# Epsilon of four norms as a third triple in VectorE's aggregate, the last norm's factor and shift side by side, and a new order of work

## The reference

```
h = patches(16x16) @ W.T + b; class token in front; + positions    # 32 x 37 tokens x 256 ("tok")
h = h + gated_scan(norm(norm0(h)))       # two norms in a row, gate = sigmoid, h_t = (1-z) h_{t-1} + z c_t, + its own input
h = h + ffn(norm1(h))                    # ternary W_fc (256->1024), exact gelu, norm with weights, ternary W_proj
h = h + attention(norm2(h))              # rope on q and k, causal softmax over 37 tokens, output product
h = h + quantised_linear(norm3(h))       # x / scale, round, clip to +-127, ternary weights, + bias
norm(x) = (x - mean) / sqrt(var + 1e-5)  # over the 256 features of a token
```

## Time and profile before

| | |
|---|---|
| median of 3 runs | 163.69 us (163.63 to 164.32) |
| profiled execution | 163.71 us, span of its instructions 161.9 us |
| TensorE busy | 148.2 us (91%) |
| VectorE | 136.1 us (84%) |
| GpSimd | 120.3 us (74%) |
| ScalarE | 109.0 us (67%) |
| mean granted clock of TensorE | 0.974 |
| chain that ended last | TensorE 70%, GpSimd 13%, VectorE 6%, waiting to issue 6% |

### The profile page before, as it was taken

The page is one execution under the profiler, slowest core; times in us unless marked ns, Lnnn a source line. Parts: engine busy times, 40 slices in busy tenths (PEclk is TensorE's granted clock), DMA queues, the critical chain, the costliest instruction groups (busy, mean ns, idle before and its releaser), DMA issues.

```text
span 161.9 us, 3532 instructions
## 1 busy us (share of the span) xinstructions
PE 148.2 (91%) x1043; PEld 129.5 (80%) x1043; DVE 136.1 (84%) x396; ACT 109.0 (67%) x264; POOL 120.3 (74%) x214
## 2 busy tenths in 40 slices
PE   7979999999998999999999999999999999697541
PEld 7969999788997887879888989988998798574220
DVE  0767679999999999999979799888988896896871
ACT  3765359736448899999998958498827637276330
POOL 1068978968927466878889988869899888988830
PEclk9999999999999999999999999999999999999955
DMA  5999992000030000000000000000000000001323
GB/s 171 340 392 392 379 417 109 4 0 2 0 130 4 2 0 2 0 4 0 0 4 2 0 4 0 2 0 0 4 0 0 0 6 2 2 10 46 87 81 81
DMA packets 6026, 10.84 MB, mean 67 GB/s; under 512 B 1841, under 2 KB 3448, under 8 KB 5752
## 3 DMA queue, kind: packets, MB, share of 16 engines
q1 hardware_dynamic: 6008, 10.62, 18.7%
HBM read 9.40 MB, written 1.21 MB: 66 GB/s over the span
## 4 chain that ended last, share of the span: by engine, by line
PE 70%; POOL 13%; DVE 6%; issue 6%; ACT 2%; DVEq 0%; ACTq 0%; POOLq 0%
PE bank L428 37%; PE bank L508 5%; PE bank L575 5%; PE bank L509 4%; PE bank L510 4%; PE bank L517 3%; POOL small L1186 3%; PE bank L435 3%; POOL qk L1251 2%; POOL small L1181 2%; POOL residual L1282 2%; POOL small L1191 2%; PE bank L549 1%; PE bank L629 1%; DVE residual L1160 1%
## 5 line engine op out<-in xcount | busy, mean ns | idle before, releaser
L1186 POOL TENSOR_TENSOR small<-small,powers 111x1 f32<-111x1 f32 (+3 forms) x55 | 33.3, 606 | 3.7
L1181 POOL TENSOR_SCALAR small<-small 111x1 f32<-111x1 f32 (+1 forms) x55 | 24.2, 441 | 15.0 <-DVE small L892 11.3
L428 PE MATMUL bank<-pj,gt_hi 128*111 128x256 f32 (+1 forms) x88 | 22.3, 293 | 0.0
L428 PE MATMUL bank<-pj,gt_lo 128*111 128x256 f32 (+1 forms) x88 | 21.3, 281 | 0.0
L1202 POOL TENSOR_TENSOR x_lo<-x_raw,x_hi 128x666 fp32r<-128x666 f32 (+1 forms) x9 | 12.8, 1434 | 10.8 <-ACT x_hi L721 10.8
L508 PE MATMUL bank<-wt_hi,x_hi 128*111 128x256 f32 (+1 forms) x66 | 19.4, 294 | 1.4 <-DVE h L998 1.1
L510 PE MATMUL bank<-wt_hi,x_lo 128*111 128x256 f32 (+1 forms) x66 | 18.6, 282 | 0.0
L509 PE MATMUL bank<-wt_lo,x_hi 128*111 128x256 f32 (+1 forms) x66 | 18.6, 282 | 0.0
L428 PE MATMUL bank<-fc,n1t_hi 128*111 128x512 f16 (+1 forms) x44 | 16.7, 380 | 0.0
L428 PE MATMUL bank<-fc,n1t_lo 128*111 128x512 f16 (+1 forms) x44 | 16.6, 378 | 0.0
L428 PEld LDWEIGHTS bank<-pj,gt_hi 128*111 128x111 f32 (+1 forms) x88 | 15.1, 171 | 0.3 <-DVE residual L1088 0.2
(11 more groups left out here) (139 smaller groups left out, 478.9 us busy)
## 6 DMA issues: line engine op xcount, KB each, us to landing
x_raw<-x_in SPq DMA_DIRECT2D x10, 333.0 KB, 6.4
w_fc<-w_fc_in SPq DMA_DIRECT2D x1, 1024.0 KB, 10.2
w_pj<-w_pj_in SPq DMA_DIRECT2D x1, 1024.0 KB, 12.2
...
```

What stands on the lines that cost most here:

```text
L428: last = mm(out, a, b, start=(n == 0), stop=(n == len(pairs) - 1))
L1181: return nc.gpsimd.tensor_scalar(small[0:rows(i), i, out:out + 1], small[0:rows(i), i, value:value + 1], factor, add, ALU.mult, ALU.add)
L1186: return gt(small[0:rows(i), i, r:r + n], small[0:rows(i), i, ve:ve + n], powers[0:rows(i), 0:n], ALU.pow)
```

## The change

Four things:
1. The statistics get a standing third triple (norm 0 a fourth, too): count 0, mean 0 and count x variance of 256 eps. The aggregate over 9 (12) values then gives var + eps at once, and the 55 additions on GpSimd go. Norm 0 has two aggregates per tile instead of one: over three triples for the inner factor, over four for the outer. The factor (1 + eps)^-1/2 that is left over goes into gamma (w_gamma on VectorE, before ScalarE's and VectorE's w_gate). The standing triples are written by five memsets on GpSimd at the start.
2. In norm 3 the shift no longer waits for the factor: it is mean x power x (-1/scale), by a second column operand, issued right behind the factor.
3. ScalarE's n3 waits for both.
4. The lists of the four engines are written anew (shown are the head and the end of each).

```diff
 ORDER = {
     "tensor": """
-        warm:0 tok:0 w_pos:0 tok:1 tok:2 tok:3 w_gate:0 tok:4 t0:0 tok:5 t0:1 tok:6 t0:2 tok:7 w_fold:0 t0:3
...
-        attend:4 turn:6 value:5 qk:11 value:6 t3:1 attend:5 turn:7 attend:6 value:7 score:8 score:9 t3:2
-        attend:7 value:8 score:10 turn:8 t3:3 t3:4 out:0 attend:8 value:9 out:1 turn:9 t3:5 attend:9 t3:6
-        turn:10 value:10 out:2 attend:10 out:3 out:4 t3:7 out:5 out:6 out:7 t3:8 out:8 t3:9 out:9 t3:10 out:10""",
+        warm:0 w_pos:0 tok:0 tok:1 tok:2 tok:3 w_gate:0 tok:4 t0:0 tok:5 t0:1 tok:6 t0:2 tok:7 w_value_bias:0
+        t0:3 t0:4 w_ternary:0 w_fold:0 w_fold:1 t0:5 gate:0 gate:1 gate:2 tok:8 t0:6 t0:7 tok:9 tok:10 gate:3
...
+        qk:6 attend:0 score:3 qk:7 value:1 turn:1 proj:10 turn:2 t2:8 value:2 t2:9 attend:1 turn:3 attend:2
+        score:4 value:3 t2:10 score:5 attend:3 qk:8 qk:9 turn:4 value:4 score:6 qk:10 attend:4 score:7 qk:11
+        turn:5 value:5 t3:0 turn:6 value:6 attend:5 turn:7 value:7 attend:6 t3:1 value:8 score:8 score:9
+        attend:7 out:0 t3:2 turn:8 score:10 attend:8 turn:9 out:1 value:9 t3:3 t3:4 attend:9 turn:10 value:10
+        out:2 t3:5 out:3 attend:10 t3:6 out:4 t3:7 out:5 out:6 t3:8 out:7 out:8 t3:9 out:9 t3:10 out:10""",
     "scalar": """
-        split:0 w_tok:0 w_tok:1 split:1 split:2 split:3 split:4 w_gate:0 split:5 split:6 split:7 w_qk:0 split:8
...
-        value:4 turn:5 n3:2 score:7 t3:0 turn:6 n3:3 value:5 value:6 value:7 turn:7 n3:4 score:8 t3:1 n3:5 t3:2
-        value:8 t3:3 turn:8 n3:6 score:9 value:9 t3:4 turn:9 n3:7 score:10 turn:10 value:10 n3:8 n3:9 t3:5 t3:6
-        t3:7 t3:8 n3:10 t3:9 t3:10""",
+        split:0 w_tok:0 split:1 w_tok:1 split:2 split:3 split:4 split:5 split:6 w_gate:0 split:7 t0:0 w_qk:0
...
+        turn:4 score:6 score:7 turn:5 value:5 turn:6 value:6 turn:7 value:7 t3:0 n3:3 n3:4 value:8 t3:1 score:8
+        turn:8 n3:5 score:9 turn:9 n3:6 t3:2 value:9 score:10 t3:3 turn:10 t3:4 n3:7 t3:5 value:10 n3:8 t3:6
+        t3:7 n3:9 t3:8 n3:10 t3:9 t3:10""",
     "vector": """
-        w_ones:0 split:0 w_tok:0 w_tok:1 split:1 split:2 w_pos:0 h0:0 stats0:0 mean0:0 w_gate:0 w_small:0 h0:1
...
-        attend:3 sinv:5 clip:0 clip:1 score:7 stats3:3 sbias:6 round:0 round:1 mean3:3 rope:4 attend:4 sbias:7
-        stats3:4 mean3:4 clip:2 rope:5 sinv:6 sinv:7 attend:5 stats3:5 attend:6 mean3:5 stats3:6 clip:3 round:2
-        score:8 score:9 sbias:8 mean3:6 round:3 attend:7 clip:4 stats3:7 sinv:8 round:4 score:10 clip:5 mean3:7
-        sbias:9 sbias:10 out:0 clip:6 attend:8 stats3:8 round:5 round:6 mean3:8 out:1 sinv:9 attend:9 clip:7
-        sinv:10 stats3:9 mean3:9 clip:8 out:2 attend:10 round:7 stats3:10 out:3 mean3:10 out:4 out:5 round:8
-        out:6 out:7 clip:9 clip:10 round:9 round:10 out:8 out:9 out:10""",
+        w_ones:0 split:0 w_tok:0 w_tok:1 split:1 w_pos:0 split:2 h0:0 stats0:0 h0:1 w_small:0 mean0:0 stats0:1
+        h0:2 stats0:2 h0:3 mean0:1 w_gamma:0 n0:0 mean0:2 w_gate_bias:0 w_gate:0 n0:1 t0:0 h0:4 stats0:3 mean0:3
...
+        score:7 stats3:4 sbias:7 mean3:4 rope:5 clip:2 round:1 round:2 sinv:6 attend:5 stats3:5 sinv:7 mean3:5
+        attend:6 clip:3 clip:4 round:3 score:8 sbias:8 stats3:6 score:9 attend:7 sbias:9 mean3:6 sinv:8 stats3:7
+        out:0 round:4 clip:5 score:10 attend:8 sbias:10 mean3:7 out:1 clip:6 round:5 sinv:9 sinv:10 stats3:8
+        mean3:8 attend:9 stats3:9 out:2 clip:7 round:6 round:7 mean3:9 out:3 attend:10 out:4 clip:8 out:5
+        stats3:10 mean3:10 round:8 out:6 out:7 clip:9 clip:10 round:9 round:10 out:8 out:9 out:10""",
     "gpsimd": """
-        w_tok:0 split:3 split:4 h0:0 split:5 split:6 h0:1 split:7 h0:2 split:8 h0:3 h0:4 h0:5 split:9 split:10
...
-        attend:0 vbias:9 rope:3 biased:0 proj:10 attend:1 vbias:10 attend:2 attend:3 biased:1 rope:4 attend:4
-        biased:2 biased:3 rope:5 attend:5 attend:6 biased:4 attend:7 attend:8 biased:5 biased:6 attend:9
-        biased:7 biased:8 attend:10 biased:9 biased:10""",
+        w_tok:0 split:3 split:4 split:5 h0:0 split:6 h0:1 h0:2 split:7 split:8 h0:3 h0:4 h0:5 h0:6 h0:7 split:9
...
+        attend:0 square:10 rope:3 proj:10 biased:0 attend:1 attend:2 biased:1 attend:3 biased:2 rope:4 vbias:9
+        attend:4 rope:5 attend:5 biased:3 biased:4 attend:6 biased:5 attend:7 vbias:10 biased:6 attend:8
+        biased:7 attend:9 biased:8 attend:10 biased:9 biased:10""",
 }
...
+SQ_EPS = LN_EPS * LN_EPS / (1.0 + LN_EPS)
+GROUP, GROUPS = 3, 4
...
-    stats = m.own("stats", [4, 2, 8], F32)
+    stats = m.own("stats", [4, 2, GROUP * GROUPS], F32)
...
+                act.wait_ge(s["gamma_ready"], 1)
                 for k in range(KD):
-                    go(wg_hi[:, k, :], w_gate[:, k, :], ACT.Copy, scale=packed[:, GAMMA + k:GAMMA + k + 1])\
+                    go(wg_hi[:, k, :], w_gate[:, k, :], ACT.Copy, scale=derived[:, D_GAMMA + k:D_GAMMA + k + 1])\
...
                 act.wait_ge(s["nb3_ready"], i + 1)
+                act.wait_ge(s["rq_ready"], i + 1)
...
-                        dve.wait_ge(s[f"mv{norm}_ready"], i - 1)
+                        dve.wait_ge(s[f"mv{norm}_ready"], (i - 1) * (2 if norm == 0 else 1))
+                    if i == 0:
+                        dve.wait_ge(s["eps_groups_ready"], 5)
...
-                    nc.vector.bn_aggr(col(i, normed[norm][2], 2), stats[0:rows(i), norm, i % 2, 0:6])\
-                        .then_inc(s[f"mv{norm}_ready"], 1)
+                    groups = stats[0:rows(i), norm, i % 2, :]
+                    if norm == 0:
+                        nc.vector.bn_aggr(col(i, MV0_SQ, 2), groups[:, 0:3 * GROUP]).then_inc(s["mv0_ready"], 1)
+                        nc.vector.bn_aggr(col(i, MV0, 2), groups[:, 0:4 * GROUP]).then_inc(s["mv0_ready"], 1)
+                    else:
+                        nc.vector.bn_aggr(col(i, normed[norm][2], 2), groups[:, 0:3 * GROUP])\
+                            .then_inc(s[f"mv{norm}_ready"], 1)
...
+            def w_gamma(_i):
+                dve.wait_ge(s["dma_packed"], 16)
+                ts(derived[:, D_GAMMA:D_GAMMA + KD], packed[:, GAMMA:GAMMA + KD], (1.0 + LN_EPS) ** -0.5, None, ALU.mult)\
+                    .then_inc(s["gamma_ready"], 1)
...
+                dve.wait_ge(s["inv_scale_ready"], 1)
+                ts(derived[:, D_NEG_INV_SCALE:D_NEG_INV_SCALE + 1], derived[:, D_INV_SCALE:D_INV_SCALE + 1], -1.0, None,
+                   ALU.mult).then_inc(s["neg_inv_scale_ready"], 1)
...
-            def scaled(i, out, value, factor, add):
-                return nc.gpsimd.tensor_scalar(small[0:rows(i), i, out:out + 1], small[0:rows(i), i, value:value + 1],
-                                               factor, add, ALU.mult, ALU.add)
-
-            def power(i, ve, r, n=1):
-
-                return gt(small[0:rows(i), i, r:r + n], small[0:rows(i), i, ve:ve + n], powers[0:rows(i), 0:n],
+            def power(i, mv, r, n=1):
+
...
+                nc.gpsimd.memset(stats[:, :, :, 2 * GROUP:3 * GROUP - 1], 0.0).then_inc(s["eps_groups_ready"], 1)
+                nc.gpsimd.memset(stats[:, 0, :, 3 * GROUP:4 * GROUP - 1], 0.0).then_inc(s["eps_groups_ready"], 1)
+                for norm, group, added in ((0, 2, SQ_EPS), (0, 3, LN_EPS - SQ_EPS)):
+                    nc.gpsimd.memset(stats[:, norm, :, GROUP * group + 2:GROUP * group + 3], D * added)\
+                        .then_inc(s["eps_groups_ready"], 1)
+                nc.gpsimd.memset(stats[:, 1:4, :, 3 * GROUP - 1:3 * GROUP], D * LN_EPS)\
+                    .then_inc(s["eps_groups_ready"], 1)
...
-                pool.wait_ge(s["mv0_ready"], i + 1)
-                scaled(i, VE0, MV0 + 1, 1.0, LN_EPS).then_inc(s["ve0_ready"], 1)
-                scaled(i, VE0 + 1, MV0 + 1, 1.0 + LN_EPS, LN_EPS * LN_EPS).then_inc(s["ve0_ready"], 1)
-                pool.wait_ge(s["ve0_ready"], 2 * i + 2)
-                power(i, VE0, R0, 2).then_inc(s["r0_ready"], 1)
+                pool.wait_ge(s["mv0_ready"], 2 * i + 2)
+                power(i, MV0, R0, 2).then_inc(s["r0_ready"], 1)
 
             def h1_(i):
                 pool.wait_ge(s["mv1_ready"], i + 1)
-                scaled(i, VE1, MV1 + 1, 1.0, LN_EPS).then_inc(s["ve1_ready"], 1)
-                pool.wait_ge(s["ve1_ready"], i + 1)
-                power(i, VE1, R1).then_inc(s["r1_ready"], 1)
+                power(i, MV1, R1).then_inc(s["r1_ready"], 1)
                 pool.wait_ge(s["r1_ready"], i + 1)
                 shift(i, NB1, MV1, R1, "nb1_ready")
 
...
                 pool.wait_ge(s["mv3_ready"], i + 1)
-                scaled(i, VE3, MV3 + 1, 1.0, LN_EPS).then_inc(s["ve3_ready"], 1)
-                pool.wait_ge(s["ve3_ready"], i + 1)
-                power(i, VE3, R3).then_inc(s["r3_ready"], 1)
+                power(i, MV3, R3).then_inc(s["r3_ready"], 1)
                 if i == 0:
                     pool.wait_ge(s["inv_scale_ready"], 1)
 
                 pool.wait_ge(s["r3_ready"], i + 1)
                 gt(small[0:rows(i), i, RQ:RQ + 1], small[0:rows(i), i, R3:R3 + 1],
```

(8 more changed lines are left out.)

103 lines of the change are left out of this document (50 added, 53 removed).

## The result

In runs side by side the changed kernel took 171.02 us in the median (168.83 to 172.12, 4 runs), the kernel before 164.00 (163.63 to 164.37, 4 runs): a ratio of 1.0345, interval 1.0244 to 1.0446. The forecast was 162.2 us in a range up to 164.5. It was wrong in sign and by 8.8 us.

A forecast was written before the change was run, and what follows sets the result against it. TensorE's products bound 12 to 130 us, latencies, mainly GpSimd's, the 32 us tail. Ideal -2.35 + 0.2 = -2.15 us, low bound -0.2; -1.5 us taken from 163.71 gave 162.2 us, range 160.9 to 164.5.

The forecast's parts named there:

- "New: idle from 6.1 to 7.9", the head at +0.5 us: Head: TensorE waits for w_pos's operands until 7.9 us, so tok:1 starts at 11.3 against 10.79, +0.5 us.
- Rival (b): Head: TensorE's gap keeps its clock low, 1.7 to 3.3 us more, giving 164.7 us; chance 0.12.
- "ScalarE's w_gate behind w_gamma and two splits. Nothing.": Head: moving ScalarE's w_gate costs nothing, as gates need wg_hi over 10 us later; without that cover, 1.5 us.
- "Between 12 and 130 us I cost their going at nothing": Middle: removing GpSimd's epsilon additions gains nothing there, since TensorE's products hide them.
- "0.2 for the late aggregates": VectorE after 30 us: three tiles' extra norm 0 aggregates are charged 0.2 us, the rest hidden.
- The aggregates: VectorE, norm 0: 11 more aggregates cost 0.8 to 1.9 us in all, 0.07 each at least; longer reads nothing.
- Rival (d): VectorE: the third triple slows 44 aggregates by up to the 0.42 us bound, +3 us or more; chance 0.03.
- The negated factor and the memsets: VectorE's small negated factor goes with the aggregates' charge; five GpSimd memsets before 2 us cost nothing.
- The tail at -2.35, taken as -1.5: Tail: GpSimd's shift of attend:10 ends at 151.65 instead of 154.00, -2.35 us; -1.5 us taken overall.
- rival (a): Tail: VectorE's attend:7 ahead of mean3:6 makes a new wait, gain only 0.2 to 0.7 us, about 163.3; chance 0.22.
- "tok:1 starts after 12": Head: sign that the prediction is wrong, if TensorE's tok:1 starts after 12 us; 11.3 was expected.
- "last shift moves by less than 1 us": Tail: sign that the prediction is wrong, if GpSimd's last shift moves less than 1 us; near 151.7 was expected.

The follow-up runs named there:

- e4: The changed kernel with GpSimd's split:9 ahead of h0:3 and ScalarE's split:10 and split:11 behind gate:0 and gate:1; 169.83 us, ratio 1.0313 to the kernel before.
- e3: The code of the kernel before on the change's four new lists, without w_gamma; 172.51 us, ratio 1.0502 to the kernel before.
- e9: The kernel before with one step moved: TensorE's w_pos:0 ahead of tok:0; 166.07 us, ratio 1.0155 to the kernel before.
- e6: The change's code on the four lists of before, w_gamma put just ahead of VectorE's w_gate; 165.19 us, ratio 1.0083 to the kernel before.
- e7: The changed kernel with the steps up to w_gate in the order of before, all behind them as changed; 169.08 us, ratio 1.0285 to the kernel before.
- e13: The change's code, w_gamma as in e10, lists of before up to w_ln_bias and the change's lists behind; 167.66 us, ratio 1.0225 to the kernel before.
- e1: The changed kernel with TensorE's w_pos:0 back behind tok:0 and ScalarE's w_tok:1 back ahead of split:1; 171.63 us, ratio 1.0469 to the kernel before.
- e10: The change's code on the lists of before, w_gamma as two one-element instructions ahead of VectorE's w_pos; 164.63 us, ratio 1.0043 to the kernel before.
- e16: e10 with GpSimd's split of tile 8 waiting for VectorE's fifth n0; 162.11 us, ratio 0.9893 to the kernel before.
- e12: e7 with GpSimd's split:9 ahead of h0:4, split:10 ahead of h0:6, and w_gamma as in e10; 166.03 us, ratio 1.0122 to the kernel before.
- e17: e12 with GpSimd's split of tile 8 waiting for VectorE's third n0; 164.30 us against 163.99 for the kernel before.
- e2: The change's code on the four lists of before, w_gamma put ahead of VectorE's h0:0; 165.6 us, ratio 1.0108 to the kernel before.

## Why the prediction was wrong, point by point

- **"New: idle from 6.1 to 7.9", the head at +0.5 us: the step that failed first.** tok:1 came at 14.05, not 11.3: +3.3 us. Of the 2.75 us that were missed, 1.3 are the landing: 7.9 was a guess from what ScalarE waited for, and sel landed at 9.19, 6.1 us behind its issue at 3.09. The other 1.4 are the clock: w_pos took 0.97 us for 0.7 and tok:0 3.84 for 2.7. In e4 sel landed as forecast, at 7.82, and tok:1 still came at 13.81, since w_pos took 1.12 and tok:0 4.83: there the clock is all of it. Rival (b) had the clock and got 12%. Its "against" (TensorE works for 5 us without a break before the gap) carried no weight: in after, e3, e4 and e9 alike, behind gaps of 2.5 to 3.2 us, the clock was down.
  Behind shorter gaps it was a matter of the execution. The same wait of 1.05 us ahead of tok:1 stands in twelve profiles: in e6, e7 and e13 the granted clock from 12 to 14 us is 0.50, in the other nine 1.00, and in e1 it is 1.00 behind 2.08 us. The Trainium skill, "TensorE: Matmul & The Clock Gate", Part 1, says that the moment at which the clock changes runs free of the kernel's start. These rows agree with it; what I drew from it in the prediction, that the change's gap would leave some executions unharmed, finds no example among the four profiles that have this gap.
- **"ScalarE's w_gate behind w_gamma and two splits. Nothing."** wg_hi came at 21.40, since w_gamma stands behind four h0 in VectorE's list, and VectorE's low half took 2.79 us for 1.60, now beside a split of GpSimd. It filled VectorE just ahead of the n0 steps. What this cost was not measured by itself in these lists.
- **"Between 12 and 130 us I cost their going at nothing": the deepest error.** The additions cost nothing there, but their going changed when GpSimd's splits start. In e10 that was a stall of 2.16 us and turned a gain into a loss; held back in e16, the same code gains 1.1%. I had asked whether GpSimd's work was hidden, not what it would start sooner and whom that would hit.
- **The order of the middle was not costed at all.** This is the largest term that was missed. I went through the edits of the head and the tail and left the stretch from 14 to 53 us at "0.2 for the late aggregates"; it cost 5.8 us. There three splits now run without a gap beside the sixth n0, which stands for 4.6 us, and the clock falls behind TensorE's wait. e7, e12 and e17 take the head and these stalls away and bring the time from 171.0 to 169.1, 166.0 and 164.3 us.
- **The aggregates: right.** 185 ns for nine values against 173, the second of a pair at 0.10 us against my 0.07. Rival (d) is out. The negated factor and the memsets cost nothing that shows. VectorE's busy time rose by 5.1 us (136.1 to 141.2), not 1 to 2, since a stall counts as busy (the sixth n0 alone 4.58 us, 1.11 before); GpSimd's fell by 20.2.
- **The tail at -2.35, taken as -1.5: half right.** The block shrank from 1.46 to 1.13 us (forecast 1.15), and counted from the last proj product qk:11 came 1.9 us earlier (10.72 against 12.60 us) and rope:5 on GpSimd 2.2 us (13.18 against 15.42), both more than worked out. But VectorE was late: mean3:10 came 28.70 us behind the last proj product, where it had come 28.05 behind, and GpSimd waited for aggregates in five places. The gain was 0.6 us. That is rival (a), a wait in the place of the one removed, within its 0.2 to 0.7; whether attend:7 ahead of mean3:6 is what made VectorE late, as it says, was not tested. With the code on old lists the gain is 1.2 to 1.5 us in five profiles, 0.5 in e2's.
- Of my tests, both bounds ("tok:1 starts after 12", "last shift moves by less than 1 us") were crossed: tok:1 at 14.05, and the last shift 8.4 us later, or 0.7 earlier if counted from the proj row. The 162.11 us of e16 is not the forecast come true: it gets there without any of the new orders.

The Trainium skill, "SBUF — State Buffer", in "SBUF: two separate sides", says that VectorE and GpSimd share a pair of ports as an exclusive lock, held for a whole instruction by whichever starts first, and that a VectorE instruction in a two-port mode needs it, or one with two operands in SBUF against a GpSimd instruction that reads SBUF. The rows agree on who is hit (the one-source centring step, the two-operand shift on one element, the one-source step on two elements, not that on one). They differ on the lock: VectorE's step began 0.52 us ahead of the split's row in e10, 0.58 ahead in the changed kernel, and still waited until the splits had ended, 1.62 and 3.85 us of them. With the same power running and the split held back (e16) it did not wait at all: its 0.15 us lie within the 0.70 of the power, which has two operands in SBUF as well. What the hardware does between a power and a split queued directly behind it is not shown here, and the profile's spans on GpSimd are rough.
